# A macaron block with routed experts: loads of picked rows moved to 15 slots behind, additions three slots ahead of the load's place, last loads back to back

## What is computed

```python
x = x + 0.5 * ffn(layernorm(x))
x = x + attn(layernorm(x))
x = x + 0.5 * ffn(layernorm(x))
# ffn: a shared expert, and the two best of eight routed experts per token
shared = silu(x @ gate) * (x @ up) @ down
probs  = sigmoid(x @ router + bias); scores, indices = top_k(probs, 2)
scores = scores / sum(scores)
out    = shared + sum over the two picks: score * expert(x)
# attn: 16 heads of 8, phi(z) = silu(z) + 1, kv = phi(k)^T v, out = phi(q) kv, then Wo
```

## Time and profile before

| What | Value |
|---|---|
| median of three runs (lowest, highest) | 775.08 us (774.51, 780.2) |
| the profiled execution's own time | 779.01 us |
| its span | 777.3 us |
| mean granted TensorE clock | 0.942 |
| busy: PE, DVE, ACT, POOL | 685.7, 549.1, 471.6, 537.2 us |
| dispatch of the first layer | about 0 to 175 us |
| first slot stage | about 172 to 368 us |
| middle | about 369 to 577 us |
| second slot stage | about 577 to 757 us |
| last loads, additions and stores | about 757 to 777 us |

### The profile page before, as it was taken

The page is one execution under the profiler, slowest core; times in us unless marked ns, Lnnn a source line. Parts: engine busy times, 40 slices in busy tenths (PEclk is TensorE's granted clock), DMA queues, the critical chain, the costliest instruction groups (busy, mean ns, idle before and its releaser), DMA issues.

```text
span 777.3 us, 17593 instructions
## 1 busy us (share of the span) xinstructions
PE 685.7 (88%) x4989; PEld 611.8 (79%) x4989; DVE 549.1 (71%) x1837; ACT 471.6 (61%) x865; POOL 537.2 (69%) x564
## 2 busy tenths in 40 slices
PE   6566878869999959999889999999989999999990
PEld 6456767759999959998667777777669999999980
DVE  7688787686555538886679987787787555576772
ACT  4346434436766737686777676766547766777750
POOL 1447777777777777777447676767777777777772
PEclk9779787989999979999999999999999999999995
DMA  8412221134364336564203111111333463567765
GB/s 265 159 41 81 78 64 51 57 114 121 99 171 129 102 107 189 172 182 120 79 28 97 45 42 46 42 44 46 86 101 107 117 171 110 148 192 225 222 194 169
DMA packets 63445, 89.65 MB, mean 115 GB/s; under 512 B 13174, under 2 KB 43768, under 8 KB 63352
## 3 DMA queue, kind: packets, MB, share of 16 engines
q1 hardware_dynamic: 46456, 53.63, 24.7%
q0 software_dynamic: 16896, 34.90, 13.3%
HBM read 46.36 MB, written 42.12 MB: 114 GB/s over the span
## 4 chain that ended last, share of the span: by engine, by line
PE 61%; DVE 17%; issue 6%; POOL 6%; DMA 5%; ACT 3%; SPq 2%; POOLq 0%; DVEq 0%; ACTq 0%
PE y_bank L1054 11%; PE y_bank L969 5%; PE g_bank L877 4%; PE u_bank L877 4%; PE g_bank L879 4%; PE u_bank L878 4%; PE g_bank L878 4%; PE u_bank L879 4%; POOL y_rows L637 4%; PE g_bank L948 3%; PE u_bank L949 2%; PE tr_bank L899 2%; DVE stats L1196 2%; POOL x_rows L625 2%; PE y_bank L1131 2%
## 5 line engine op out<-in xcount | busy, mean ns | idle before, releaser
L625 POOL DMA_INDIRECT x_rows<-send,send_to x256 | 249.7, 975 | 133.3 <-issue 69.5
L637 POOL DMA_INDIRECT y_rows<-send,y_to x272 | 267.2, 982 | 84.5 <-issue 69.7
L1682 DVE TENSOR_TENSOR h<-silu_g,u_bank 128x512 f32<-128x512 f32 x136 | 93.3, 686 | 115.6 <-ACT silu_g L780 111.5
L755 ACT ACTIVATE slot_gu<-w_gu 128x1024 fp32r x130 | 137.8, 1060 | 40.6 <-issue 33.8
L1054 PE MATMUL y_bank<-w_dn,h 128*128 x1088 | 144.2, 276 | 0.5 <-DVE x L1274 0.4
L1054 PEld LDWEIGHTS y_bank<-w_dn,h 128*128 128x128 f32 x1088 | 133.5, 192 | 0.9 <-issue 0.9
L877 PE MATMUL g_bank<-xT_hi,slot_gu 128*128 128x256 f32 x260 | 85.0, 327 | 9.1 <-DVE xT_lo L1673 7.3
L969 PEld LDWEIGHTS y_bank<-w_dn,h 128*128 128x128 f32 x512 | 67.3, 206 | 28.0 <-issue 26.8
L969 PE MATMUL y_bank<-w_dn,h 128*128 128x128 f32 x512 | 68.2, 291 | 17.9 <-DVE x L1274 17.9
L780 ACT ACTIVATE silu_g<-g_bank 128x512 f32<-128x512 f32 x136 | 78.9, 580 | 7.5 <-PE g_bank L879 6.8
L877 PE MATMUL u_bank<-xT_hi,slot_gu 128*128 128x256 f32 x260 | 73.3, 282 | 0.0
(11 more groups left out here) (258 smaller groups left out, 1468.1 us busy)
## 6 DMA issues: line engine op xcount, KB each, us to landing
send<-x_rows SPq DMA_DIRECT2D x130, 130.0 KB
y_pair<-y_rows SPq DMA_DIRECT2D x32, 512.0 KB
y_rows<-send,y_to POOLq DMA_INDIRECT x272
x<-x_in SPq DMA_DIRECT2D x16, 256.0 KB, 7.1
x_rows<-send,send_to POOLq DMA_INDIRECT x256
out<-x SPq DMA_DIRECT2D x16, 256.0 KB
w_raw<-w_experts SPq DMA_DIRECT2D x15, 256.0 KB, 3.5
x_rows<-pad SPq DMA_DIRECT2D x16, 130.0 KB
```

What stands on the lines that cost most here:

```text
L625: pool.indirect_dma_start(x_rows, bass.IndirectOffsetOnAxis(ap=send_to[b % SEND_TO_RING][:, w, k:k + 1], axis=0), send[ring_of(f, t)][:, w ...
L637: pool.indirect_dma_start(y_rows, bass.IndirectOffsetOnAxis(ap=y_to[k][:, j:j + 1], axis=0), result_rows(f, s)[:, j, :], None).then_inc(y_ ...
L755: act.activation(slot_gu[n % 2][:].rearrange("p a n -> p (a n)"), w_gu[:, bass.ds(e, 1)].rearrange("p e a n -> p (e a n)").bitcast(F32), A ...
L1682: dve.tensor_tensor(h[par][0][:], silu_g[par][:], u_bank[par][:], ALU.mult).then_inc(slot_h_done, 1)
```

## The change

The constants `LEAVE` become 15 and 9. The place of an addition is three less than that of its load (`AHEAD_OF_ADD`); a load stands at least `ROW_RING` + 1 = 7 behind the addition of the tile before the last. Stores stand six behind the first addition. Behind the last slot of the second stage, the tail's stores are interleaved with loads 12 and 13 only, and loads 14 and 15 follow each other directly.

```diff
-LEAVE = (10, 8)
-BETWEEN = 5
+LEAVE = (15, 9)
+AHEAD_OF_ADD, STORE_LEAVE = 3, 6
...
-                loads.append(max(last_slot(f, t) + LEAVE[f], adds[t - Y_RING] + BETWEEN if t >= Y_RING else 0))
-                adds.append(max(loads[t], adds[t - 1] + 2 if t else 0))
+                loads.append(max(last_slot(f, t) + LEAVE[f], adds[t - Y_RING] + ROW_RING + 1 if t >= Y_RING else 0))
+                adds.append(max(loads[t] - AHEAD_OF_ADD, adds[t - 1] + 2 if t else 0))
...
-                stores = [t for t in range(tiles) if first_add(f, t) + LEAVE[f] - 3 < slots] if f else []
+                stores = [t for t in range(tiles) if first_add(f, t) + STORE_LEAVE < slots] if f else []
...
-                for t in range(len(loads), tiles):
-                    load_picks(f, t)
-                    if f and t - Y_RING >= len(stores):
-                        store_tile(t - Y_RING)
-            for t in range(tiles - Y_RING, tiles):
+                if f == 0:
+                    for t in range(len(loads), tiles):
+                        load_picks(f, t)
+            stored_tiles = len(stores)
+            for t in range(len(loads), tiles):
+                load_picks(1, t)
+                while t < tiles - Y_RING and stored_tiles < t:
+                    store_tile(stored_tiles)
+                    stored_tiles += 1
+            for t in range(stored_tiles, tiles):
                 store_tile(t)
```

More of the change, by code:

```diff
@@ L564, in _ @@
                     for t in stores:
-                        if first_add(f, t) + LEAVE[f] - 3 == s:
+                        if first_add(f, t) + STORE_LEAVE == s:
                             store_tile(t)
-                for t in range(len(loads), tiles):
-                    load_picks(f, t)
-                    if f and t - Y_RING >= len(stores):
-                        store_tile(t - Y_RING)
-            for t in range(tiles - Y_RING, tiles):
+                if f == 0:
[8 more added lines that the diff above has]
+            for t in range(stored_tiles, tiles):
                 store_tile(t)
```

## The result

| | before | changed |
|---|---|---|
| median | 776.62 us (13 runs, 774.51 to 780.2) | 783.57 us (13 runs, 780.6 to 787.21) |
| profiled execution: span, mean clock | 777.3 us, 0.942 | 782.3 us, 0.945 |

What follows compares the result with a forecast made beforehand. PE was taken to set the pace, 2.52 us a slot. First-stage wait and clock +1.0, second-stage additions +4.6 and tail -0.8 gave +4.8 on the median of 775.08: 779.9 us, range 772 to 787.

Steps and rivals of the forecast that it cites:

- forecast case: The prediction's main case, whole kernel: 779.9 us, within 777 to 782.8, chance 0.6.
- part 2: Second stage: additions three slots ahead of the load's place make DVE wait, +6.0 us there, +4.6 at the end.
- Part 1, the wait: First stage: PE's 8.78 us wait near 280 goes, the stage ends 7 us earlier, lost at the seam behind POOL.
- Part 1, the clock: Seam between the stages: PE idles 7.8 us and its clock falls again, costing 1.2 us, between 0 and 1.8.
- Part 2, the load's price: Second stage: a load of picked rows takes 4.0 us from issue to landing, bounds 3.31 and 4.6.
- the prediction's own loop: Second stage, tiles two slots apart: 0.96 to issue, 4.0 load, 1.09 to next results; 6.05 us against 5.04.
- Part 2, POOL absorbs 1.4: Second stage: a slower pace lets POOL catch up by 1.4 us, so +6.0 becomes +4.6 at the end.
- Part 3: Tail: load 15 goes 0.43 us behind load 14 instead of 1.30, -0.8 us.
- The gain survives: Rival: the 7 to 10.6 us gained in the first stage reach the end; about 768 us, chance 0.06.
- Loads land in time: Rival: second-stage loads take about 3.31 us, so early additions cost only 0.5; 775 us, chance 0.2.
- The loop decides: Rival: second-stage loads take 4.6 us or more, sharing DMA engines; +8.5 in sum, 783.6 us, chance 0.14.
- The change doesn't remove the wait: Rival: first stage, SP would still wait 1 us for slot 30's send; worth 0.5 us, counted within the forecast.

Runs made afterwards that it cites:

- the moved `rstd`: Changed kernel with POOL's `rstd` of tile 0 moved from behind the last send to between the sends of slots 64 and 65: 776.14 us, ratio 1.0009.
- the first stage with the tail: First stage and tail as in the changed kernel, second stage's places as in the kernel before: 777.91 us, ratio 1.0008 against the kernel before.

## Why the prediction was wrong, and where it was right

The direction, the order of the parts and their mechanisms held. The size did not: 4.8 us forecast and 7.0 measured, and 783.57 lies beyond the forecast case's own 777 to 782.8, in the part above it to which the prediction gave 0.14. The step that failed is a term of part 2, the 4.0 us for a load of picked rows: the loads took 4.34 in the mean. With it the prediction's own sum is 1.0 + 6.7 - 0.8 = +6.9. Of the 3.7 us between 779.9 and 783.57, 1.5 are the median of before, which was 775.08 in three runs and is 776.62 in thirteen; 2.1 are mine. The prediction also took about 1% as the least that a measurement tells from no change; the interval of the ratio is 0.3% wide, so that 0.9% is clear of it.

For the profiled execution the prediction said 783.8, and it was 784.07. That is luck: the changed kernel's was 1.34 us ahead before the change could act. With the offset the two executions (784.07 and 779.01) are 6.4 us apart: +0.9 up to slot 30 of the second stage (forecast +1.0), +6.4 from there to POOL's last send (forecast +4.6) and -0.9 behind it (forecast -0.8). The other 0.6 of the 7.0 lies between this pair of executions and the medians.

- **Part 1, the wait** (10.6 us, 3.5 given back to the additions, 7 left): right. The stage is 6.9 us shorter, and what was given back shows in PE's waits for `xT_lo` between 292 and 369 us, 5.5 us instead of 1.7. That POOL's last send stays and that `shift` then waits some 8 us: right, 8.64, and shown by the moved `rstd`, which lets some 7 us through.
- **Part 1, the clock** (+1.2): right in the traced execution, where the stretch behind `shift` is 1.1 us longer. But that was the light case. In the three other kernels with a long pause there (7.3 to 9.8 us) it is 3.1 to 3.3 longer in the one execution traced of each, which goes beyond my bound of 1.8. It fits the first stage with the tail, +0.9 on the median where +0.2 was forecast, though that run's interval holds both.
- **Part 2, the load's price** (4.0 us, bounds 3.31 to 4.6): this is the step that failed. For tiles 4 to 9 the changed kernel's loads took 4.08, 5.31, 4.07, 3.93, 4.63 and 4.01 us from issue to addition, 4.34 in the mean. The chain of waits has those of tiles 8 and 9:
```profile
721.83 4.61 DMA y_pair<-y_rows
...
728.50 3.99 DMA y_pair<-y_rows
```
  Put into the prediction's own loop, 0.96 + 4.34 + 1.09 = 6.39, it gives +1.35 a tile, +8.1 in the stage and +6.7 behind POOL; the trace has +7.2 in results from slot 30 to slot 65 and +6.4 at POOL's last send (769.54 against 763.61, from an offset of -0.4). The loop itself is right. In the changed kernel with the moved `rstd`, SP's timeline has the loads of tiles 4 and 9 here, five rounds apart:
```profile
688.23 0.38 SPq L524 DMA_DIRECT2D y_pair<-y_rows  x1
...
720.01 0.38 SPq L524 DMA_DIRECT2D y_pair<-y_rows  x1
```
  31.78 / 5 = 6.36 us a round, with loads of 4.6, 4.14, 4.5, 4.08 and 4.24 us: 0.96 + 4.31 + 1.09 = 6.36. I had put the load under the one row of its kind (4.27), because its store no longer stands right behind it. The mean of six in a row came out over that row. That they share the DMA engines with sends and rows (DMA share 0.66 between 676 and 757 us) may be why; no run varies it. The prediction adds 0.61 us for the product of slot 35, where the row has 0.69; with that a load could take 3.7 us instead of 3.6, which moves no term of the sum.
- **Part 2, POOL absorbs 1.4**: right, 1.2.
- **Part 3** (-0.8): about right, though load 15 goes 0.77 us behind load 14 and not 0.43. From POOL's last send to the span's end are 782.3 - 769.5 = 12.8 us instead of 13.7. The time alone can't show it: the old places with the tail and `rstd` moved came to 0.9997, and the interval holds both -0.8 and nothing.
- **The rivals.** *The gain survives*: it does not here, but the moved `rstd` shows how little stood in its way. *Loads land in time*: fallen, 4.34 against the estimate of 3.2 us by the Trainium skill's page "DMA: Bandwidth & Descriptors", section "Anatomy of one DMA". That section is on DMAs that GpSimd issues, and SyncE issues these. *The loop decides* had the number, 783.6, with a load of 4.6 us; its mechanism is the forecast's with one input larger, and since each 0.1 us of load is worth 0.6 us at the end, the two should have been weighed as one case with a price between 4.0 and 4.6. *The change doesn't remove the wait*: fallen, PE has no such wait any more.

## What to carry to other kernels

Where a consumer was put "ahead" of its load in a table of places, compare when each engine reaches its place, in us, not in slots: one slot (2.5 us) decided over 7 us here. When such a loop repeats, an error in the transfer's price is multiplied by the rounds, so take the price from several loads of that stretch, and not from the one row that fits best. And before a stall is removed, look one stage on for what is queued behind work that the stall never touched; here a single small POOL instruction behind 74 sends swallowed 7 us, and moving it past six of them gave them back.

## What the runs showed that I had not expected

- **Much the same pause, two prices of the clock.** After 8.49 us of idling PE was back at full speed 4.6 us after its restart in the changed kernel. With the additions two slots ahead, PE's timeline at the same place:
```profile
376.67 1.22 PE L1123 MATMUL y_bank<-attn_raw,kv_sb 128*128 128x128 f32 x4 [9.76 <-DVE kv_sb L1759]
...
385.46 2.06 PE L1106 MATMUL g_bank<-pad,attn_raw 128*128 128x512 f32 x2
...
389.01 1.06 PE L904 MATMUL tr_bank<-ident,xn 128*128 128x128 f32 x4
...
391.06 1.10 PE L953 MATMUL g_bank<-pad,shared_raw 128*128 128x512 f32 x2
```
  It stays at the lower level (two matmuls of 512 columns in 2.06 us, 1.10 later) until about 390, 13 us. The two other kernels with a pause of 7.3 and 7.6 us did so too. The instructions of PE there are the same in all four. And in the best kernel (additions two slots ahead, `rstd` moved) pauses of 1.02 and 1.25 us were enough, while the changed kernel with the moved `rstd` had much the same ones (1.03 and 1.24 us) and kept the full clock (1.00 in 372 to 384). Table of stretches of the best one:
```profile
366.00:372.00 6.00, 4.92 (x31) 3.79 (x30) 3.81 (x10) 4.69 (x11) 3.05 (x3) 1.00 0.07 23
372.00:378.00 6.00, 4.80 (x19) 3.63 (x19) 2.81 (x6) 3.29 (x8) 4.62 (x5) 0.66 0.46 142
378.00:384.00 6.00, 6.00 (x24) 4.97 (x24) 4.96 (x24) 2.42 (x5) 1.23 (x2) 0.50 0.33 102
```
  It cost 2.4 us (213.1 instead of 210.7 in the table above), and 2.5 in the first stage with `rstd` moved (213.2).

  What decides stays open, and it need not be the kernel: each trace is one execution, and the executions of one kernel differ as much. Of the kernel with the first stage and the tail, three took 773.99 to 774.28 us at a mean clock of 0.947 to 0.949, and nine, the traced one among them, 777.66 to 780.1 at 0.938 to 0.947. Of the best kernel the traced execution had 0.945, the five faster ones 0.950 to 0.955. No trace shows where the faster ones gained.
- **The new places, one slot looser, are better than the old ones** by about 2 us: 165.8 to 166.6 us in the second stage against 167.7 to 169.1, and 2.0 and 1.8 us between the medians of the two pairs. The intervals of each pair overlap, and no run takes this apart.
- **A chip on which the same kernel takes 995 us**, 28% more. DVE's, ACT's and POOL's main instructions have the same durations within about 1%; PE's down products (L1059) take 291 ns in the mean instead of 275, at a mean clock of 0.879 instead of 0.941, and the waits between engines are longer (PE for `xT_lo` at L882 in the whole kernel 64.1 us instead of 10.3, first stage and tail changed). The second stage's new places cost nothing there: PE's pace no longer sets that stage. The changed kernel itself was not run on it.
